# The router slabs' correction in an attention and mixture kernel: first row loaded ready-made, base and rows by other queues, expert 7 loaded last

## What is computed

```python
logits = (h @ router_w.T + router_b).reshape(T, O, E)
probs = softmax(logits)
w, sel = top_k(probs, 2); w = w / sum(w)
c[t, sel[t, o]] += w[t, o]
expert_out = einsum('th,eoh->teo', h, expert_w) + expert_b
final = einsum('te,teo->to', c, expert_out)
```

## Time and profile before

| | |
|---|---|
| Median of 3 runs | 2001.44 us (1998.28 to 2002.37) |
| Profiled execution | 2001.44 us, span 1999.7 us |
| TensorE busy | 1917.4 us, 96% |
| VectorE, ScalarE, GpSimd busy | 1434.9, 1038.1, 866.1 us |
| Stages, in the span | attention to about 661 us, router to 1289, experts to the end |

### The profile page before, as it was taken

The page is one execution under the profiler, slowest core; times in us unless marked ns, Lnnn a source line. Parts: engine busy times, 40 slices in busy tenths (PEclk is TensorE's granted clock), DMA queues, the critical chain, the costliest instruction groups (busy, mean ns, idle before and its releaser), DMA issues.

```text
span 1999.7 us, 30398 instructions
## 1 busy us (share of the span) xinstructions
PE 1917.4 (96%) x9756; PEld 1515.9 (76%) x9756; DVE 1434.9 (72%) x2841; ACT 1038.1 (52%) x2061; POOL 866.1 (43%) x1028
## 2 busy tenths in 40 slices
PE   4999999999996999999999999899999999999999
PEld 3667766777763788788888888688888888888887
DVE  5677667767658758788888888477777777777732
ACT  2566566566554347777777877443344333334400
POOL 3687777777677235355454435101231111122100
PEclk8899999999997999999999999999999999999999
DMA  5454554455456477776766455822232223223111
GB/s 164 112 124 128 144 143 125 125 148 138 102 157 205 167 247 243 235 257 233 249 215 228 172 201 194 303 87 84 79 112 103 79 80 99 79 79 124 55 42 32
DMA packets 103549, 294.54 MB, mean 147 GB/s; under 512 B 13761, under 2 KB 14785, under 8 KB 98338
## 3 DMA queue, kind: packets, MB, share of 16 engines
q1 hardware_dynamic: 92354, 211.80, 33.1%
q10 hardware_dynamic: 7776, 65.01, 10.0%
q0 software_dynamic: 3328, 16.78, 3.7%
HBM read 150.31 MB, written 109.16 MB: 130 GB/s over the span
## 4 chain that ended last, share of the span: by engine, by line
PE 88%; DVE 4%; ACT 2%; POOL 2%; issue 2%; DMA 1%; SPq 0%; ACTq 0%; DVEq 0%; POOLq 0%
PE pair L260 22%; PE pair L262 22%; PE pair L261 22%; PE pair L668 4%; PE ps L714 4%; PE pair L701 3%; PE ps L260 3%; PE ps L261 3%; PE ps L262 3%; PE ps L734 1%; DVE pair L1354 1%; ACT pT L1070 1%; PE ps L891 1%; DVE nmax L1348 1%; DMA lg_all<-ev_a 1%
## 5 line engine op out<-in xcount | busy, mean ns | idle before, releaser
L260 PE MATMUL pair<-w_h,hT 128*128 128x512 f32 x1920 | 751.4, 391 | 8.5 <-DVE w_l L1657 8.5
L261 PE MATMUL pair<-w_l,hT 128*128 128x512 f32 x1920 | 748.2, 390 | 0.0
L262 PE MATMUL pair<-w_h,hT 128*128 128x512 f32 x1920 | 748.2, 390 | 0.0
L1854 POOL TENSOR_TENSOR logits<-logits,second 128x512 f32<-128x512 f32 x224 | 298.4, 1371 | 595.6 <-DVE second L1565 595.4
L260 PEld LDWEIGHTS pair<-w_h,hT 128*128 128x128 f32 x1920 | 361.1, 188 | 83.0 <-issue 8.9
L262 PEld LDWEIGHTS pair<-w_h,hT 128*128 128x128 f32 x1920 | 361.1, 188 | 75.8
L261 PEld LDWEIGHTS pair<-w_l,hT 128*128 128x128 f32 x1920 | 361.2, 188 | 74.1
L1668 DVE SCALAR_TENSOR_TENSOR xb<-pair,c_all,xb 128x512 f32<-128x512 f32 x256 | 191.7, 749 | 198.8 <-PE pair L262 192.8
L1070 ACT ACTIVATE pT<-pair,zero 128x1024 f32<-128x1024 f32 (+3 forms) x256 | 202.7, 793 | 196.2 <-PE pair L701 193.1
L1354 DVE CUSTOM_DVE_ANT_0 pair<-pair,future 128x256 f32<-128x256 f32 (+3 forms) x340 | 184.3, 554 | 122.2 <-PE pair L668 114.0
L1164 ACT ACTIVATE w<-tree 128x512 f32<-128x512 f32 x32 | 20.3, 635 | 395.6 <-DVE tree L1567 395.6
(11 more groups left out here) (160 smaller groups left out, 2619.1 us busy)
## 6 DMA issues: line engine op xcount, KB each, us to landing
logits<-lg_all ACTq DMA_DIRECT2D x32, 1792.0 KB, 8.8
qk_st<-qk SPq DMA_DIRECT2D x384, 128.0 KB, 2.3
lg_all<-ev_a SPq DMA_DIRECT2D x33, 768.0 KB, 8.3
lg_all<-ev_b SPq DMA_DIRECT2D x31, 768.0 KB, 4.5
xb<-x SPq DMA_DIRECT2D x64, 256.0 KB, 3.0
hT_all<-hT SPq DMA_DIRECT2D x32, 512.0 KB, 4.3
hT<-hT_all SPq DMA_DIRECT2D x32, 512.0 KB, 4.1
xt<-in_x SPq DMA_DIRECT2D x8, 1024.0 KB, 5.5
```

The costliest lines, as they stand in the source:

```text
L260: pe.matmul(dst, lh, rh, start=start, stop=False)
L261: pe.matmul(dst, lh, rl, start=False, stop=False)
L262: return pe.matmul(dst, ll, rh, start=False, stop=stop)
L1854: pool.tensor_tensor(logits[t % 2][:, e - 1, :], logits[t % 2][:, e - 1, :], second[:], ALU.subtract)\
```

## The change

The first row comes ready-made: GpSimd adds the slab's own first row to the bias difference in batch 0 (`rows_first`), so that the ordinary correction gives the bias row, and the copy L1493 goes (`FIXES` 4). A slab is then loaded in three transfers (`load_raw`): chunks 1 to 3, rows 1 to 127 of chunk 0, and row 0 from `rows_first`. The base and rows of slabs 0 to 2 are issued by ScalarE at step (2, 0), one transfer per row; those of 3 to 6 by SyncE in the epilogue behind slab 6, when the last sums are done. Slab 3 is corrected in `fix_rest`, and some places in memory move. At the hand-over logits 3 to 5 of the last tile go to `ev_b`, and expert 7 is loaded last, when both stores are done.

```diff
-        ones = att("ones", [P, HD], F32)
-        free_at = att.at
...
+        ones = att("ones", [P, HD], F32)
...
-        rows_e = ffn("rows_e", [P, EARLY, 2, O], F32, at=raw_at + slot * (NE + 2))
-        base_e = ffn("base_e", [P, KC, O], F32, at=raw_at + slot * (NE + 2) + 8 * EARLY * O)
-        rows_l = ffn("rows_l", [P, ND - EARLY, 2, O], F32, at=raw_at + slot * (NE + 5) - 4 * O)
-        base_l = ffn("base_l", [P, KC, O], F32, at=free_at)
+        base_e = ffn("base_e", [P, KC, O], F32, at=raw_at + slot * (NE + EARLY))
+        row_e = ffn("row_e", [P, EARLY, O], F32, at=raw_at + slot * (NE + EARLY + 1))
+        logits_at = ffn.at
+        row_l = ffn("row_l", [P, ND - EARLY, O], F32, at=logits_at)
+        base_l = ffn("base_l", [P, KC, O], F32, at=logits_at + 4 * (ND - EARLY) * O)
...
-        rows_bias = nc.dram_tensor("rows_bias", [ND, O], F32, kind="Internal").ap()
+        rows_first = nc.dram_tensor("rows_first", [ND, O], F32, kind="Internal").ap()
...
-        FIXED = ((0, 6), (0, 7), (2, 0), (2, 1), (2, 7), (3, 0))
-        FIXES = 5
-        FIX_EARLY = {(2, 5): ((0, 0),), (2, 6): ((0, 1), (0, 2)), (2, 7): ((0, 3), (0, 4)),
-                     (3, 0): ((1, 0), (1, 1)), (3, 1): ((1, 2), (1, 3), (1, 4)), (3, 3): ((2, 0), (2, 1)),
-                     (3, 4): ((2, 2), (2, 3), (2, 4)), (3, 6): ((3, 0), (3, 1)), (3, 7): ((3, 2), (3, 3), (3, 4))}
+        FIXED = ((0, 6), (0, 7), (2, 1), (2, 7), (3, 0), (3, 2))
+        BASE_STEP = (2, 0)
+        FIXES = 4
+        FIX_EARLY = {(2, 5): ((0, 0),), (2, 6): ((0, 1), (0, 2)), (2, 7): ((0, 3),), (3, 0): ((1, 0), (1, 1)),
+                     (3, 1): ((1, 2), (1, 3)), (3, 3): ((2, 0), (2, 1)), (3, 4): ((2, 2), (2, 3))}
...
-        RAW_BASE = routerT[:, 0, :].rearrange("(c p) o -> p c o", p=P)
...
-        def raw_router(k):
...
-            return routerT[:, k + 1, :].rearrange("(c p) o -> p c o", p=P)
...
-        def spread(rows):
...
-            return rows.rearrange("k o -> () k o").broadcast_to([P, rows.shape[0], O])
+        RAW_PARTS = 3
...
+        def load_raw(queue, k):
...
+            done = s[f"fix{k}_in"]
+            queue.dma_start(w_raw[:, k, 1:KC], routerT[P:H, k + 1, :].rearrange("(c p) o -> p c o", p=P)).then_inc(done, 16)
+            queue.dma_start(w_raw[1:P, k, 0], routerT[1:P, k + 1, :]).then_inc(done, 16)
+            queue.dma_start(w_raw[0:1, k, 0], rows_first[k:k + 1, :]).then_inc(done, 16)
...
             def body(b, first, more, further):
...
-                    if not more and c >= 2:
-                        load_corrections(c)
...
-                        sp.dma_start(rows_bias, bias_row[0:ND, :]).then_inc(s["prep_out"], 16)
...
-            def load_corrections(c):
...
-                sp.wait_ge(s["shifted"], (NB - KC + c) * UNITS)
-                rows, base, ks, done = ((rows_e, base_e, slice(0, EARLY), s["base_in"]) if c == 2 else
-                                        (rows_l, base_l, slice(EARLY, ND), s["late_in"]))
-                if c == 2:
-                    sp.dma_start(base[:], RAW_BASE).then_inc(done, 16)
-                sp.dma_start(rows[:, :, 1, :], spread(rows_less[ks, :])).then_inc(done, 16)
-                sp.dma_start(rows[0:1, :, 0, :], rows_bias[ks, :].rearrange("k o -> () k o")).then_inc(done, 16)
-                if c == 3:
-                    sp.wait_ge(s["summed"], NB - 1)
-                    sp.dma_start(base[:], RAW_BASE).then_inc(done, 16)
+                        sp.dma_start(rows_first, bias_row[0:ND, :]).then_inc(s["prep_out"], 16)
...
-                sp.dma_start(w_raw[:, ND - 1], raw_router(ND - 1)).then_inc(s[f"fix{ND - 1}_in"], 16)
+                load_raw(sp, ND - 1)
+                sp.wait_ge(s["summed"], NB)
+                sp.dma_start(base_l[:], routerT[:, 0, :].rearrange("(c p) o -> p c o", p=P)).then_inc(s["late_in"], 16)
+                for k in range(EARLY, ND):
+                    sp.dma_start(row_l[:, k - EARLY], rows_less[k:k + 1, :].broadcast_to([P, O])).then_inc(s["late_in"], 16)
...
             def load_expert(e):
+                if e == 0:
+                    sp.wait_ge(s["fix_erows"], 16)
...
-            sp.wait_ge(s["fix_erows"], 16)
-            sp.wait_ge(s["lg_out_b"], t * 16)
-            load_expert(ND)
...
-                if e == 2:
+                if e == 3:
...
-            store_logits(t, "b", 6, ev_a[:], 3, 6)
+            store_logits(t, "b", 6, ev_b[:], 3, 6)
...
+            sp.wait_ge(s["lg_out_a"], NT * 16)
+            sp.wait_ge(s["lg_out_b"], NT * 16)
+            load_expert(ND)
...
-                act.dma_start(w_raw[:, k], raw_router(k)).then_inc(s[f"fix{k}_in"], 16)
+                load_raw(act, k)
...
+            def load_base():
+                act.dma_start(base_e[:], routerT[:, 0, :].rearrange("(c p) o -> p c o", p=P)).then_inc(s["base_in"], 16)
+                for k in range(EARLY):
+                    act.dma_start(row_e[:, k], rows_less[k:k + 1, :].broadcast_to([P, O])).then_inc(s["base_in"], 16)
...
+                        if last and (c, v) == BASE_STEP:
+                            load_base()
...
             def hi_expert(e):
...
-                if e == ND:
-                    act.wait_ge(s["lg_out_b"], NT * 16)
...
             def copy_logits(t, k):
...
-                if t == NT - 1 and k == 3:
-                    act.wait_ge(s["lg_out_a"], NT * 16)
-                elif k in (0, 3, 6):
+                if k in (0, 3, 6):
...
-                dst = ev_c[:] if k == 6 else (ev_a, ev_a if t == NT - 1 else ev_b)[k // 3][:, k % 3, :]
+                dst = ev_c[:] if k == 6 else (ev_a, ev_b)[k // 3][:, k % 3, :]
...
-                    dve.wait_ge(s[f"fix{k}_in"], 16)
+                    dve.wait_ge(s[f"fix{k}_in"], RAW_PARTS * 16)
...
-                        dve.wait_ge(s["base_in"], 3 * 16)
+                        dve.wait_ge(s["base_in"], (1 + EARLY) * 16)
...
-                        dve.wait_ge(s["late_in"], 3 * 16)
-                rows, base, j = (rows_e, base_e, k) if k < EARLY else (rows_l, base_l, k - EARLY)
+                        dve.wait_ge(s["late_in"], (1 + ND - EARLY) * 16)
...
+                    base = base_e if k < EARLY else base_l
...
-                elif q < 4:
+                else:
...
-                    row = rows[:, j, 1:2, :].broadcast_to([P, KC // 2, O])
-                    dve.tensor_tensor(w, w, row, ALU.add).then_inc(s["fw_fix"], 1)
-                else:
-                    dve.wait_ge(s["fw_fix"], k * FIXES + 3)
-                    dve.tensor_copy(w_raw[0:1, k, 0, :], rows[0:1, j, 0, :]).then_inc(s["fw_fix"], 1)
+                    row = row_e[:, k:k + 1] if k < EARLY else row_l[:, k - EARLY:k - EARLY + 1]
+                    dve.tensor_tensor(w, w, row.broadcast_to([P, KC // 2, O]), ALU.add).then_inc(s["fw_fix"], 1)
             def fix_rest():
                 def whole(k):
...
+                whole(3)
...
-                               ALU.subtract).then_inc(s["prep_ok"], 1)
+                               ALU.subtract).then_inc(s["prep_row"], 1)
+            pool.wait_ge(s["prep_row"], 1)
+            pool.tensor_tensor(bias_row[router_rows, :], bias_row[router_rows, :], own_row[router_rows, :],
+                               ALU.add).then_inc(s["prep_ok"], 1)
...
```

More of the change, by code:

```diff
@@ L207, in build @@
             logs recips refined o_ok o_hi o_lo wo_mm x1_ok xr_in0 xr_in1 x1_out0 x1_out1
-            fw_hi fw_lo prep_in prep_ok prep_out base_in late_in fw_fix fixed fix_erows one_ok xb_in ln2_st ln2_var ln2_rs ln2_nm ln2_nb hn_ok
+            fw_hi fw_lo prep_in prep_row prep_ok prep_out base_in late_in fw_fix fixed fix_erows one_ok xb_in ln2_st ln2_var ln2_rs ln2_nm ln2_nb hn_ok
             hT_mm hT_hi hT_lo lg_mm lg_ok lg_out_a lg_out_b lg_out_c lg_in0 lg_in1 top gap_ok th_ok second_ok u_ok w2_ok count first_step c_sum c_half c_ok
```

## The result

The changed kernel takes 2053.65 us (median of 4 runs, 2052.13 to 2055.13) against 2000.72 before on the same chip (4 runs): ratio 1.0266, 95% interval 1.0248 to 1.0284. It is slower, as forecast, but by 53 us and not 24: the time lies above the range of 2006 to 2048. The profiled execution took 2050.08 us. From here, "later" and "earlier" are within the span.

What follows compares the result with a forecast made beforehand. TensorE, 96% busy, was taken as the bound, so only its idle stretches could change. The sum was 2001.4 + 27.3 (router pairs late through one DMA engine) - 3.9 (hand-over) = 2025 us, range 2006 to 2048.

Steps and rivals of the forecast that it cites:

- Equal parts, one share: Slab loads: a transfer is cut only into equal shares, so 127 rows go to one DMA engine, 10.2 us; given 85%.
- The formula for `fix_rest`: After the last attention batch: corrections, splits, statistics and slabs 5 and 6 end the router pairs no sooner than F + 38.4.
- F: Start of `fix_rest`, held by the stores of `x1`: 663.95 us before, forecast about 690.
- ScalarE's issues: Base and row issues at (2, 0), about 0.4 us each beside the exponentials: no cost, or up to 0.5 us.
- Rival (b): Starved small transfers: shift rows and residual loads 10 us late, issues stall; +42 us, 2040 or more; chance 0.18.
- The term F from the backlog: Last batch: 1360 packets, 109 us on engine 0 from 576, delay the `x1` stores; router pairs end 27 us later.
- Slab 3 and the mask: Last attention batch: without slab 3's corrections GpSimd's mask comes 5.5 us earlier; 4.4 us gained if loads are in time.
- Hand-over: Router to experts: 8.5 us wait and 2 of clock saved, 4.6 and 2 back at expert 7; net 3.9.

Runs made afterwards that it cites:

- even: Changed kernel with the 127 rows of chunk 0 loaded as rows 1 to 15 and rows 16 to 127: 1995.77 us, ratio 0.9976 to before.
- 61-row: Changed kernel with the 127 rows loaded as two transfers of 66 and 61 rows: 2022.61 us, ratio 1.0109 to before.
- shape-alone: Kernel before with only its seven slab loads changed to the changed kernel's three parts: 2057.27 us, ratio 1.0294.
- single-row-first kernel: Changed kernel with the one-row transfer issued ahead of the 127-row one: 2032.19 us, ratio 1.0166 to before.

## Why the prediction was wrong

**Right.** The direction and its cause, the cut of the 127 rows. Equal parts, one share (given 85%), a packet of 80 ns (77 measured), DMA share near 0.07 with slabs under way. Shown by the even, the 61-row and the shape-alone kernels. The Trainium skill, "DMA: Bandwidth & Descriptors", section "Why a DMA increments its semaphore by 16 and not by 1", states 127 partitions on one engine; the runs agree, and for 61 rows too. The formula for `fix_rest` held as well: pairs end at F + 38.4 was given, 750.28 - 711.25 = 39.0 came.

**The step that failed is *ScalarE's issues*:** "nothing for them where the queue is free, up to 0.5 where it isn't". The row behind each 127-row transfer took a median of 9.7 us of ScalarE, six times; ScalarE idled 52.7 us behind issues between 560 and 800, and TensorE's wait for exponentials grew by 45.1. By this, TensorE was late in the batch itself, which the forecast left untouched. The forecast had put the whole loss into F through the backlog: F = 690, where 711.25 came, 47.3 and not 26 later than before. Rival (b) named the mechanism ("on ScalarE that stops exponentials"), with 18%, but built its price on shift rows that come 10 us late, with 3.02 us as its only row for a long issue. Its numbers lie nearer than the forecast's (F near 705, pairs at 743, 2040 or more), but in part by luck: the wait for `nm_l` that was to be its mark did not grow (3.9 us in all, 4.2 before). The working that was missing: a transfer of 127 packets on one engine takes 10.2 us, three transfers are issued back to back, and the third can't be assumed free while the second stands on the same engine. As an estimate from the prediction's own packet price, six slabs by 10.2 us are 61 us; that end belonged in the range, which stopped at 2048.

**The term F from the backlog** was also mis-sized in itself, because it treated engine 0 as busy from 576 without gaps while attention went on at its old pace. Attention was slowed by the holds, so its last transfers were issued 36 us later; then the epilogue's own backlog (slab 6, base, rows) put 11.3 us on the stores of `x1`. Only this last part has the mechanism that the forecast gave to the whole, and 4.6 us of it are SyncE's own long issues ahead of the landing. One of its signs failed with it: TensorE was to idle some 25 us between router slabs 2 and 3, and idles 9.2 (722.72). (In the sum 728.4 - 701.2 is 27.2, not 27.3; it changes nothing.)

**Slab 3 and the mask.** That GpSimd's `oT_l` is slow beside VectorE's corrections of slab 3 was read rightly (8.17 us there, 1.26 without them; the waits for the mask fell by 10.0 us in the changed kernel, and by 5.1 with slab 3 moved alone), but the forecast's 4.4 us did not come: alone the move gave nothing in the median and 2.4 us at the end of the pairs. In the changed kernel it could not pay, since F hung on the stores.

**Hand-over.** Forecast 3.9 us net (bounds 0 and 10.5); alone it gave 2.7 (interval 0.6 to 5.0). Expert 7's wait in the changed kernel was 5.2 in place of 4.6; store b took 12.7 us from the start of its issue until the load could go. The mechanism was right, the size a little off.

**Sum, with what was measured.** Before 2000.7; shape of the slabs + 57.7 (from the shape-alone kernel, 2057.27 - 1999.58); moves and hand-over - 3.8 (even kernel, 1995.77 - 1999.58): 2054.6, against 2053.65.

**Open.** Why the issue behind is held for nearly the whole 127-row transfer on ScalarE's queue (6.8 to 10.8 us), and only 4.2 us on SyncE's for the same shape at 688.17. On SyncE the next five issues are long too (base and four rows 6.7 us, 2.5 in the even kernel), so its hold may only be spread over more of them. Nor does a hold end with the transfer: ScalarE is free at 597.7, and one engine alone stays busy (DMA share 0.06 to 0.07) until about 606. How much backlog an issue is let through with is not shown. No run here varies the queue alone. Nor do the runs split the backlog's part exactly from that of the holds; the single-row-first kernel gives some 20 us as what order alone is worth.

## What to carry to other kernels

Read a transfer's row count as a divisor question before anything else: cut off one row of 128, and 127 rows lie on one engine; cut it as 15 and 112, and nothing is lost here. When a transfer is slow, price its issuer as well as its data: if the issuing engine computes (here ScalarE's exponentials), the issues behind the slow one stop it, and everything that waits for it. A store that gates a buffer's reuse should be issued by the engine that fills the buffer, not behind 3 MiB of loads in another queue; here that gave 4.9 us (1999.07 - 1994.18).

## What the runs showed of the hardware

- The hold falls on an issue behind a one-engine transfer, not on that transfer: 0.59 us for the first slab's 127 rows, 10.14 for the single row after them. With the order turned, the 127 rows take 0.28 (median), and the next slab's issues up to 7.3.
- A one-row transfer of 2 KB took 0.31 us to issue behind 112 evenly shared rows, with nearly the same bytes issued: what held the issues here was the backlog of one engine, not the queue's bytes.
- With 61 rows on one engine the issue behind the first slab's took 0.41 us and the one behind the second's, 3.0 us later, 13.2. Read as backlog that adds up over slabs; no run varies the gap alone.
- A wait that was removed from attention's end came back within 50 us, since the engine whose work had filled it (VectorE) had that work to do later: 7.2 us gained at the mask, 2.4 left at the end of the router pairs, none in the median.
